# Softmax attention on one core: the value product of a unit behind its four scores, whole instead of in two halves

## The chip, the cores and the metric

The program runs on one core of a Trainium2 chip. The metric is the device time of one execution in microseconds (us). The kernel before took 858.94 us, the median of three runs (858.55 to 862.60). Engines: PE is TensorE, DVE VectorE, ACT ScalarE, POOL GpSimd, SP SyncE, which issues the DMAs.

## The reference, cut to what matters

A two-layer model over x of 2 x 1024 tokens of 128 numbers: linear attention, a mixture of experts, softmax attention, a second mixture. The change lies in the third part:

```
q = rope(x @ Wq.T + bq); k = rope(x @ Wk.T + bk); v = x @ Wv.T + bv     # 16 heads of 8
attn = softmax(q @ k.T / sqrt(8), axis=-1)                               # 1024 x 1024 per head
x = x + (attn @ v) @ Wo.T + bo
```

## The kernel before

The four parts follow each other with a barrier between; the third is `attn1`, one function per engine. It goes through 8 sets (`st`: 2 batches x 4 groups of 4 heads). A **unit** u is one set's block of 128 keys (`kb`, 8 of them) against one half of the queries (`qh`, 512 of them): 16 units a set, 128 in all.

Two streams run side by side.

*Maxima.* For each **tile** (one head, 128 queries) PE multiplies the queries with all 1024 keys in two matmuls of 512 columns into two neighbouring banks (`max_half`, L932), and DVE takes the maximum of the 1024 (`max_tile`, L1063). Even tiles use banks 3 and 4, odd ones 5 and 6; tile n waits until the maximum of n-2 is taken. There are 256 tiles: 22 (`AHEAD`) before the units, then two beside each unit (`tiles_before`), up to unit 116. In the text A and B are the two tiles of a unit, A0, A1, B0, B1 their halves.

*Scores and values.* For each unit PE makes four scores, one per head (`scores`, L961, s0 to s3 in the text), each 128 keys x 512 queries into one bank. The row that carries minus the maximum is part of the operands. ACT takes the exponential into `a1_p` (L1201), which holds three units. Two units later PE multiplies the exponentials with the values (`values`, L974): float32, four heads into four column groups of bank 7, accumulated over the 8 blocks of keys. Each float32 matmul shows as two records, so a call shows as eight. At the first of the 8 blocks PE waits until ACT has copied the last sum out of bank 7 (L1214; ACT does that behind the four exponentials of a unit u with u % 8 = 1, once the product issued in that unit is done).

*Banks of the scores.* Score i of the list `TAKEN` takes bank i % 3 until `FIVE` (the scores of units up to 117), and waits for the exponential that read that bank before (`free_bank`, L937): that of i-3. Behind `FIVE` there are five banks. Once in eight units (u % 8 = 6) the turned rows of maxima (`turn_rows`, L950) take a place in the same list between s1 and s2; ACT copies them (L1192) and a DMA puts them in place.

*Order.* Each engine runs its instructions in the order written. PE's order in a unit is that of the loop at L1003 to L1015: A0 s0 A1 s1, first value half of unit u-2, the turned rows where there are any, B0 s2 B1 s3, second value half. Without tiles (units 117 to 127) it is s0 s1, the whole product, s2 s3. `project_out` (L979) waits for DVE, which turns the outputs (`turn`, `turn_back`) when all maxima are taken. ACT also does a few casts for the last projections (L1141, L1148) behind units 0, 2, 9 and 10.

Of the kernel before, what the change touches and what calls it, by code (L numbers as in the profile page):

```python
# [827 lines left out]
def bank_of(i):  # L828

    return i % 3 if i < FIVE else ((5, 6) + tuple((FIVE + k) % 3 for k in range(3)))[(i - FIVE) % 5]  # L830
# [54 lines left out]
def tiles_before(u):  # L885

    return [n for n in (2 * u + AHEAD, 2 * u + AHEAD + 1) if n < TILES]


def attn1_pe(c):  # L890
# [25 lines left out]
    def max_half(n, half):  # L916
        g, qh, h, qt = tile_at(n)
        k, bank = g % NG, 3 + 2 * (n % 2)
        if half == 0:
            if n == 0:  # L920
                pe.wait_ge(S("a1_b6"), 1)
                pe.wait_ge(S("a1_first"), 3 * 16)
            if n == 1:
                pe.wait_ge(S("a1_b5"), 1)
            if n == 16:
                pe.wait_ge(S("a1_second"), 16)
            if n >= 32 and n % 32 == 0:
                pe.wait_ge(S(f"a1_one{g}"), 3 * 16)
            if n >= 2:
                pe.wait_ge(S("a1_red"), n - 1)  # L930
        rows = slice(S1B, S1B + KR)
        mm = pe.matmul(ps[:, bank + half, :], q[rows, k, qh, h, qt * P:(qt + 1) * P],  # L932
                       kk[rows, k, h, half * BLK:(half + 1) * BLK], start=True, stop=True)
        if half == 1:
            mm.then_inc(S("a1_s1"), 1)

    def free_bank(i):  # L937
        if before_in_bank(i) is not None:
            pe.wait_ge(S("a1_exp"), before_in_bank(i) + 1)
        elif i >= FIVE:  # L940
            pe.wait_ge(S("a1_red"), TILES)

    def turn_rows(e):
        i = TAKEN["rows", e]
        pe.wait_ge(S("a1_split"), e + 1)
        if e == 0:
            pe.wait_ge(S("a1_b4"), 1)
            pe.wait_ge(S("a1_b7"), 1)
        free_bank(i)
        pe.matmul(ps[0:3 * HG * 4, bank_of(i), 0:P], m["a1_ms"][:].rearrange("p i a -> p (i a)"), m["a1_id"][:],  # L950
                  start=True, stop=True).then_inc(S("a1_s2"), 1)

    def scores(u, h):
        st, qh, kb = u // U, u % U // NTB, u % NTB
        k, i = st % NG, TAKEN["score", u * HG + h]
        if h == 0 and u % U == 0:
            pe.wait_ge(S(f"a1_two{st}"), 3 * 16)
        if h == 0 and kb == 0:
            pe.wait_ge(S(f"a1_mrow{qh}"), 16 * (st + 1))
        free_bank(i)  # L960
        pe.matmul(ps[:, bank_of(i), :], kk[0:KA, k, h, kb * P:(kb + 1) * P],  # L961
                  q[0:KA, k, qh, h, :], start=True, stop=True).then_inc(S("a1_s2"), 1)

    def values(u, half=None):
        st, qh, kb = u // U, u % U // NTB, u % NTB
        at = slice(0, BLK) if half is None else slice(half * (BLK // 2), (half + 1) * (BLK // 2))
        if half != 1:
            if kb == 0:
                pe.wait_ge(S("a1_va"), st + 1)
                if u >= NTB:  # L970
                    pe.wait_ge(S("a1_o"), u // NTB)
            pe.wait_ge(S("a1_exp"), TAKEN["score", u * HG + HG - 1] + 1)
        for h in range(HG):
            mm = pe.matmul(ps[32 * h:32 * h + 32, 7, at], va[:, kb, (st % NG) * HG + h, :],  # L974
                           pt[:, (u % 3) * HG + h, at], start=kb == 0 and half != 1, stop=kb == NTB - 1, skip_group_check=True)
        if half != 0:
            mm.then_inc(S("a1_pv"), 1)

    def project_out(b):  # L979
        pe.wait_ge(S("a1_back"), b + 1)  # L980
        pe.wait_ge(S("a1_exp"), max((i + 1 for i in range(FIVE, len(TAKEN)) if bank_of(i) == 3 + b), default=1))
        for j in range(TPB):
            mm = pe.matmul(ps[:, 3 + b, j * D:(j + 1) * D], xnT[:, (b * TPB + j) * P:(b * TPB + j + 1) * P],
                           m["a1_wo"][:], start=True, stop=True)
        mm.then_inc(S("a1_out"), 1)
# [17 lines left out]
    for u in range(G * U):  # L1003
        beside = tiles_before(u)
        for i, n in enumerate(beside or (None, None)):
            for half in range(2):
                if n is not None:
                    max_half(n, half)
                scores(u, 2 * i + half)
            if u >= 2 and (beside or i == 0):  # L1010
                values(u - 2, i if beside else None)
            if i == 0 and u % NTB == NTB - 2 and u + 2 < G * U:
                turn_rows((u + 2) // NTB)
        if u in OUT_UNITS:
            project_out(OUT_UNITS[u])  # L1015
    values(G * U - 2)
# [384 lines left out]
def attn1(c, w, x):  # L1401
    attn1_sp(c)
    attn1_pe(c)
    attn1_act(c, x)
    attn1_dve(c, x)
    attn1_pool(c, x)
    tables_sp(c, w, "f1", 1)
    c.sp.wait_ge(c.sem("n_row"), NT * (c.turn + 1) + TPB)
    c.sp.wait_ge(c.sem("a1_nrow"), 2 * TPB)
    rows_out_sp(c, "f1", 1, range(3))  # L1410
# [1234 lines left out]
```

## Time and profile before

| | before |
|---|---|
| median of the runs | 858.94 us |
| the profiled execution: time | 860.77 us |
| its span, first to last instruction | 859.0 us |
| mean granted clock of TensorE | 0.903 |
| PE busy | 715.8 us (83%) |
| DVE busy | 658.8 us (77%) |
| ACT busy | 526.6 us (61%) |
| POOL busy | 238.3 us (28%) |

The span is the time from the first to the last instruction of the profiled execution; durations in the trace come from it. The units run from about 448 to 752 us. Starts and durations are in us; a row of the timeline merges instructions of one line that follow each other without a gap and gives their number as x2, x3. In brackets stands the idle time of the engine before the row and what ended it. Matmuls are pipelined: the next one starts before the record of the last one ends, so the distance of two starts is the price, not the duration. A granted clock of 1.00 is 2.4 GHz, one of 0.50 is 1.2 GHz.

### The profile page before, as it was taken

How to read it: one execution, taken by the hardware profiler on the slowest of the kernel's cores; microseconds unless marked ns; L12 is line 12 of the kernel's file. 1: busy time of each engine (PE TensorE's matmuls, PEld its weight loads, DVE VectorE, ACT ScalarE, POOL GpSimd, SP SyncE). 2: the span in 40 equal slices, each digit the busy share in tenths (PEclk: the TensorE clock that was granted, in tenths of full speed). 3: DMA queues.
4: the chain of work that ended last, by engine and by line, in shares of the span. 5: the costliest groups of instructions: out<-in, count | busy, mean ns of one | idle time of the engine just before them, and what ended most of it. 6: DMA issues, size and time to landing. Idle time of an engine off the chain costs nothing. (4 is left out here: it accounts for less than half of the span.)

```text
span 859.0 us, 20505 instructions
## 1 busy us (share of the span) xinstructions
PE 715.8 (83%) x8024; PEld 359.3 (42%) x8024; DVE 658.8 (77%) x1317; ACT 526.6 (61%) x1028; POOL 238.3 (28%) x295
## 2 busy tenths in 40 slices
PE   5999978887736999963989999999999999946880
PEld 2333236553426999961412222222222222236770
DVE  7887985446875555537799999999999999664555
ACT  3763622365713444425629999999999999624453
POOL 0130010204216767552473300100000100006773
PEclk9999989997856999985958999999999999767995
DMA  3440010000082311221756650403300000032123
GB/s 101 98 100 3 1 24 5 4 3 1 0 302 95 110 48 50 38 61 60 205 129 148 170 126 2 88 16 75 73 16 2 2 2 9 4 128 84 50 50 101
DMA packets 40968, 55.47 MB, mean 65 GB/s; under 512 B 9210, under 2 KB 31234, under 8 KB 40490
## 3 DMA queue, kind: packets, MB, share of 16 engines
q1 hardware_dynamic: 36906, 46.04, 20.1%
q0 software_dynamic: 3968, 8.13, 3.5%
q8 instruction: 64, 1.05, 0.5%
q14 instruction: 30, 0.25, 0.1%
HBM read 35.22 MB, written 14.55 MB: 58 GB/s over the span
## 5 line engine op out<-in xcount | busy, mean ns | idle before, releaser
L1063 DVE TENSOR_REDUCE arena<-psum 128x1 f32<-128x1024 f32 x256 | 292.8, 1217 | 10.4 <-PE psum L932 10.4
L1201 ACT ACTIVATE arena<-psum 128x512 f32<-128x512 f32 x512 | 276.5, 597 | 18.7 <-PE psum L961 11.4
L932 PE MATMUL psum<-arena 56*128 56x512 bf16 x512 | 164.5, 404 | 4.7 <-DVE arena L1063 3.6
L974 PE MATMUL psum<-arena 128*32 128x256 f32 (+1 forms) x1944 | 163.4, 408 | 5.9 <-issue 5.9
L961 PE MATMUL psum<-arena 59*128 59x512 bf16 x512 | 158.4, 390 | 0.1
L369 PE MATMUL psum<-arena 128*128 128x128 f32 x808 | 108.1, 281 | 0.4 <-DVE arena L420 0.4
L369 PEld LDWEIGHTS psum<-arena 128*128 128x128 f32 x808 | 102.0, 198 | 0.7 <-DVE arena L420 0.7
L974 PEld LDWEIGHTS psum<-arena 128*32 128x32 f32 x1944 | 38.8, 108 | 107.5 <-issue 61.6
L932 PEld LDWEIGHTS psum<-arena 56*128 56x128 bf16 x512 | 28.9, 95 | 115.6 <-DVE arena L1063 97.9
L485 POOL DMA_INDIRECT rows_y<-arena x62 | 62.6, 1009 | 37.7 <-DVE arena L434 31.9
L396 PE MATMUL psum<-arena 128*128 (+1 forms) x496 | 66.5, 277 | 2.8 <-ACT arena L464 2.0
L480 POOL DMA_INDIRECT arena<-rows_x,arena x62 | 60.0, 968 | 26.0 <-issue 17.4
L1273 POOL TENSOR_SCALAR arena<-arena 128x16 f32<-128x16 f32 x16 | 4.1, 254 | 220.4 <-DVE arena L1063 220.3
L396 PEld LDWEIGHTS psum<-arena 128*128 128x128 f32 x496 | 60.3, 192 | 4.8 <-issue 3.3
L461 ACT ACTIVATE arena<-psum 128x512 f32<-128x512 f32 x39 | 23.3, 597 | 44.1 <-PE psum L369 44.1
L453 ACT COPY arena<-arena 128x512 f32 x39 | 24.1, 618 | 32.0 <-PE psum L369 19.4
L2300 PE MATMUL psum<-arena 128*32 128x512 f32 x352 | 41.2, 593 | 0.2 <-DMA arena<-arena 0.2
L424 DVE TENSOR_TENSOR arena<-arena,psum 128x512 f32<-128x512 f32 x39 | 26.8, 687 | 18.4 <-PE psum L369 18.4
L961 PEld LDWEIGHTS psum<-arena 59*128 59x128 bf16 x512 | 30.6, 94 | 17.3 <-ACT arena L1201 14.2
L434 DVE COPY arena<-psum 128x128 f32<-128x128 f32 x62 | 18.1, 292 | 25.0 <-PE psum L396 13.5
L2040 ACT ACTIVATE arena<-psum 128x64 f32<-128x64 f32 x32 | 7.2, 225 | 44.7 <-PE psum L2322 44.7
L417 DVE COPY arena<-arena 128x512 f32 x39 | 17.0, 437 | 19.2 <-issue 16.2
(314 smaller groups left out, 1059.5 us busy)
## 6 DMA issues: line engine op xcount, KB each, us to landing
arena<-scr_q SPq DMA_DIRECT2D x32, 224.0 KB
arena<-scr_k SPq DMA_DIRECT2D x15, 448.0 KB
arena<-in_f_up SPq DMA_DIRECT2D x1, 4096.0 KB, 14.0
arena<-rows_y SPq DMA_DIRECT2D x12, 256.0 KB, 4.8
scr_q<-arena SPq DMA_DIRECT2D x6, 384.0 KB, 5.3
arena<-in_f_down SPq DMA_DIRECT2D x1, 2048.0 KB, 17.0
arena<-in_f_up SPq DMA_DIRECT2D x1, 2048.0 KB, 9.4
rows_x<-xn SPq DMA_DIRECT2D x5, 256.0 KB, 13.0
```

Source lines behind the costliest of these rows:

```text
L369: mm = pe.matmul(ps[:, bank, f * P:(f + 1) * P], w[:, a.pair, at], xt[:, a.pair, :], start=True, stop=True)
L396: mm = pe.matmul(ps[:, 5 + 2 * d.pair, 0:P], h[:, d.pair, f * P:(f + 1) * P], merged(wdown[:, ed, f * P:(f + 1) * P]), start=f == 0, stop= ...
L424: dve.tensor_tensor(h[:, u.pair, :], sg[:, u.pair, :], ps[:, 2 + u.pair, :], ALU.mult).then_inc(hidden, 1)
L453: act.copy(m["e_w"][:, x0.pair, F:2 * F], merged(m["e_up"][:, bass.ds(e, 1), F:2 * F])).then_inc(picked2, 1)
L480: pool.indirect_dma_start(xs[:, t % GATHERED, :], None, src, index).then_inc(landed[t % GATHERED], 16)
L485: pool.indirect_dma_start(dst, index, y[:, d.slot, :], None).then_inc(stored[d.slot], 16)
L932: mm = pe.matmul(ps[:, bank + half, :], q[rows, k, qh, h, qt * P:(qt + 1) * P], kk[rows, k, h, half * BLK:(half + 1) * BLK], start=True, s ...
L961: pe.matmul(ps[:, bank_of(i), :], kk[0:KA, k, h, kb * P:(kb + 1) * P], q[0:KA, k, qh, h, :], start=True, stop=True).then_inc(S("a1_s2"), 1)
L974: mm = pe.matmul(ps[32 * h:32 * h + 32, 7, at], va[:, kb, (st % NG) * HG + h, :], pt[:, (u % 3) * HG + h, at], start=kb == 0 and half != 1 ...
L1063: dve.tensor_reduce(mx[:, qh, h * 4 + qt:h * 4 + qt + 1], ps[:, bank:bank + 2, :].rearrange("p a b -> p (a b)"), X, ALU.max).then_inc(S("a ...
L1201: act.activation(pt[:, (u % 3) * HG + h, :], ps[:, bank_of(i), :], ACT.Exp, scale=float(HD) ** -0.5).then_inc(S("a1_exp"), 1)
L2300: mm = pe.matmul(ps[32 * h:32 * h + 32, fir_bank(n, i), :], m["a0_wfir"][:, (g0 + g) * H0 + h, :], v4[:, h, b, PAD + t0 - 4 * g:PAD + t0 - ...
```

## The change

In the loop of PE the call of `values` moves behind the loop over the two tiles, and it is made without a half. In each unit PE first issues the matmuls of both tiles' maxima and all four scores (with the turned rows between the two tiles, where there are any), then the value product of unit u-2 with 512 columns: four float32 matmuls instead of eight of 256 columns. In the units without maxima the product was whole already; it moves from behind s1 to behind s3. ACT, DVE, POOL and SP are unchanged, and so are all waits.

```diff
@@ -1007,10 +1007,10 @@
                 if n is not None:
                     max_half(n, half)
                 scores(u, 2 * i + half)
-            if u >= 2 and (beside or i == 0):
-                values(u - 2, i if beside else None)
             if i == 0 and u % NTB == NTB - 2 and u + 2 < G * U:
                 turn_rows((u + 2) // NTB)
+        if u >= 2:
+            values(u - 2)
         if u in OUT_UNITS:
             project_out(OUT_UNITS[u])
     values(G * U - 2)
```

## Rows read from the trace of the kernel before

**Rows 1.** The page's groups: line, engine, count | busy us, mean ns | idle before
```profile
L1063 DVE TENSOR_REDUCE arena<-psum 128x1 f32<-128x1024 f32 x256 | 292.8, 1217 | 10.4 <-PE psum L932 10.4
L1201 ACT ACTIVATE arena<-psum 128x512 f32<-128x512 f32 x512 | 276.5, 597 | 18.7 <-PE psum L961 11.4
L932 PE MATMUL psum<-arena 56*128 56x512 bf16 x512 | 164.5, 404 | 4.7 <-DVE arena L1063 3.6
L974 PE MATMUL psum<-arena 128*32 128x256 f32 (+1 forms) x1944 | 163.4, 408 | 5.9 <-issue 5.9
L961 PE MATMUL psum<-arena 59*128 59x512 bf16 x512 | 158.4, 390 | 0.1
```

**Rows 2.** Stretches: window, length, busy per engine (x), granted clock, DMA, GB/s
```profile
573.00:591.40 18.40, 18.02 (x197) 4.55 (x193) 18.21 (x17) 17.88 (x35) 1.09 (x5) 1.00 0.52 102
...
609.80:628.20 18.40, 18.02 (x197) 4.55 (x193) 18.21 (x17) 17.88 (x35) 1.09 (x5) 1.00 0.48 102
```

**Rows 3.** Timeline of PE, unit 72 to the start of 73: start, us, instruction
```profile
615.95 0.39 PE L961 MATMUL psum<-arena 59*128 59x512 bf16 x1
616.17 0.38 PE L961 MATMUL psum<-arena 59*128 59x512 bf16 x1
616.48 0.64 PE L974 MATMUL psum<-arena 128*32 128x256 f32 x8
617.05 0.39 PE L961 MATMUL psum<-arena 59*128 59x512 bf16 x1
...
618.16 0.39 PE L961 MATMUL psum<-arena 59*128 59x512 bf16 x1
```

**Rows 4.** Timeline, ACT and DVE in the same unit: exponential of s0, two maxima
```profile
616.38 0.60 ACT L1201 ACTIVATE arena<-psum 128x512 f32<-128x512 f32 x1
...
615.51 2.35 DVE L1063 TENSOR_REDUCE arena<-psum 128x1 f32<-128x1024 f32 x2
615.51 1.22 DVE L1063 TENSOR_REDUCE arena<-psum 128x1 f32<-128x1024 f32 x1
```

**Rows 5.** Timeline of unit 70, which has the turned rows
```profile
611.27 0.39 PE L961 MATMUL psum<-arena 59*128 59x512 bf16 x1
611.70 1.08 ACT L1201 ACTIVATE arena<-psum 128x512 f32<-128x512 f32 x2
612.20 0.59 ACT L1201 ACTIVATE arena<-psum 128x512 f32<-128x512 f32 x1
612.84 0.09 PEld L961 LDWEIGHTS psum<-arena 59*128 59x128 bf16 x1 [0.19 <-ACT arena L1201]
612.84 0.39 PE L961 MATMUL psum<-arena 59*128 59x512 bf16 x1
613.16 0.64 PE L974 MATMUL psum<-arena 128*32 128x256 f32 x8
613.73 0.39 PE L961 MATMUL psum<-arena 59*128 59x512 bf16 x1
614.37 1.23 DVE L1063 TENSOR_REDUCE arena<-psum 128x1 f32<-128x1024 f32 x1
```

**Rows 6.** Timeline of unit 114: ACT copies bank 7, PE's value half waits
```profile
712.41 0.39 PE L961 MATMUL psum<-arena 59*128 59x512 bf16 x1
712.70 0.59 ACT L1214 COPY arena<-psum 128x512 f32<-128x512 f32 x1
713.17 0.63 ACT L1201 ACTIVATE arena<-psum 128x512 f32<-128x512 f32 x1
713.39 0.64 PE L974 MATMUL psum<-arena 128*32 128x256 f32 x8 [0.38 <-issue]
715.07 0.39 PE L961 MATMUL psum<-arena 59*128 59x512 bf16 x1
```

**Rows 7.** Timeline: s0 of unit 3, s0 of unit 117
```profile
456.72 0.39 PE L961 MATMUL psum<-arena 59*128 59x512 bf16 x1
...
719.50 0.60 PE L961 MATMUL psum<-arena 59*128 59x512 bf16 x2
```

**Rows 8.** Timeline, unit 117: a whole value product; DVE's last maximum
```profile
719.14 1.22 DVE L1063 TENSOR_REDUCE arena<-psum 128x1 f32<-128x1024 f32 x1
720.03 1.06 PE L974 MATMUL psum<-arena 128*32 128x512 f32 x8
721.03 1.03 PE L961 MATMUL psum<-arena 59*128 59x512 bf16 x4
```

**Rows 9.** Timeline, units 10 and 11: ACT's casts for the last projections
```profile
472.76 0.62 ACT L1141 CAST arena<-arena 128x512 bf16<-128x512 f32 x1
473.96 0.64 PE L974 MATMUL psum<-arena 128*32 128x256 f32 x8 [0.90 <-issue]
475.94 0.62 ACT L1148 CAST arena<-arena 128x512 bf16<-128x512 f32 x1
```

**Rows 10.** Timeline of PE in unit 121: the wait for DVE's turned outputs
```profile
731.05 1.16 PE L983 MATMUL psum<-arena,xnT 128*128 128x128 f32 x8 [1.11 <-DVE xnT L1096]
```

**Rows 11.** Stretches (columns as in rows 2): early units, and behind unit 121
```profile
448.00:456.00 8.00, 7.42 (x33) 1.46 (x32) 7.44 (x7) 5.89 (x12) 1.84 (x2) 0.50 0.98 217
456.00:470.00 14.00, 14.00 (x155) 3.71 (x153) 13.81 (x13) 13.67 (x27) 6.07 (x9) 0.99 0.44 116
470.00:480.00 10.00, 9.10 (x104) 2.35 (x96) 9.30 (x9) 9.82 (x20) 2.32 (x2) 1.00 0.90 218
731.00:744.00 13.00, 12.95 (x53) 4.36 (x54) 12.38 (x40) 5.70 (x12) 0.00 (x0) 0.61 0.00 0
```

**Rows 12.** All waits ended by L1201: us in total, times
```profile
PEld psum L974: 45.3, 106
PEld psum L961: 14.2, 28
```

**Rows 13.** Timeline at clock 0.50: score and exponential, whole product and next score
```profile
453.15 0.60 PE L961 MATMUL psum<-arena 59*128 59x512 bf16 x1
453.79 0.60 ACT L1201 ACTIVATE arena<-psum 128x512 f32<-128x512 f32 x1
736.33 1.93 PE L974 MATMUL psum<-arena 128*32 128x512 f32 x8
738.20 0.60 PE L961 MATMUL psum<-arena 59*128 59x512 bf16 x1
```

## The prediction

> **What bounds the kernel now.** I read the page's groups first [rows 1]. Nearly all of the attention stage is five groups: one maximum per tile on DVE (L1063), four exponentials per unit on ACT (L1201), and on PE the matmuls of maxima (L932), scores (L961) and values (L974). The table of stretches [rows 2] shows DVE, ACT and PE all at 97% to 99% of three successive 18.40 us stretches at a granted clock of 1.00, so busy shares can't say which of them sets the pace; the starts can.
>
> One unit of before runs so [rows 3]. A maxima matmul and a score matmul start together (they use different rows of the array), the second pair 0.22 us later, the value half 0.31 after that, and the next pair 0.57 after the half. That is 1.10 to 1.11 us a tile and 2.21 a unit (s0 of unit 72 at 615.95, of unit 73 at 618.16). DVE repeats in 2.35 - 1.22 = 1.13 us, 2.26 a unit, so PE pulls slowly ahead of it. But in each eight units PE loses time twice: the unit with the turned rows lasts 2.46 (611.27 to 613.73, [rows 5]), and the unit behind an output eviction 2.67, since the first half waits for the copy out of bank 7 (712.41 to 715.07, [rows 6]). Six units of 2.21 and these two make 18.4 us (stretches of that length repeat in every count and busy time, [rows 2]); DVE needs only 16 x 1.13 = 18.1 of it. So PE's order of work is the bound now, with DVE 0.3 us in 18.4 behind it and ACT (4 x 0.49 = 1.96 a unit; two that follow at once last 1.08, so the second starts 1.08 - 0.59 = 0.49 behind the first, [rows 5]) farther back. Units 3 to 116 take from 456.72 to 719.50 = 262.8 us [rows 7]. By parts: 86 ordinary x 2.21 + 14 x 2.46 + 14 x 2.67 = 261.9, and 0.5 to 0.6 for the two units beside ACT's last splits.
>
> **PE's own work falls.** Eight value matmuls of 256 columns become four of 512. The price of a whole one stands in the trace, since the units without maxima already use it [rows 8]: 0.31 after the last score it starts, and 1.00 later the next score starts (720.03 to 721.03). PE's work in an ordinary unit is then 3 x 0.23 + 0.31 + 1.00 = 2.00 us against 2.21. By the Trainium skill, "TensorE: Matmul & The Clock Gate", section "Back-to-back issue gap", two gaps of 256 columns (262 cycles each) would equal one of 512 (518), so halving would be free; the rows have 1.00 against 2 x 0.57 and they decide. If PE's own work were all, the unit would drop to DVE's pace.
>
> **What the new order adds is a wait.** Until FIVE the scores use three banks in turn, so score i waits for the exponential of score i-3. With the halves between them, four scores were spread over the unit and only the unit with turned rows waited. Now the fourth score s3 must wait for the exponential of s0 of its own unit, and s0 starts only behind the previous whole product, which stands behind the previous s3. PE works in order, so this is a closed ring, one unit long:
> - s3 to its value product: 0.32 (a score that has waited, 612.84 to 613.16, [rows 5])
> - value product to the next s0: 1.00 [rows 8]
> - s0 to its exponential: 0.43 (615.95 to 616.38, [rows 3, 4])
> - that exponential: 0.60 [rows 4]
> - its end to the score that waits for it: 612.84 - (612.20 + 0.59) = 0.05 [rows 5]
>
> Sum 2.40 us a unit. It is longer than PE's work (2.00) and DVE's pace (2.26), so it sets the pace. s3 would be ready 0.68 after s0 and starts 1.08 after it.
>
> Behind the waiting s3 on PE are the whole value product and then both maxima of the next unit; DVE waits for those. B1 is ahead of s3 and isn't held up. A ring over DVE exists too: B0, B1 0.23, values 0.31, next A0 1.00, its maximum 0.64 (lead of A0 over its reduction, 713.73 to 714.37, [rows 5]), the next 1.13, that one's 1.22 and 0.05 of release: 4.58 over two units, 2.29 each, under 2.40. ACT's wait for a free third of a1_p (values of u-3) ends 1.06 + 0.04 behind the start of the previous product, while the new s0's result is there 1.43 behind it: hidden by 0.3.
>
> **The two special units.** Turned rows take a bank too, so in these 14 units (6, 14, ... 110) s3 waits for the exponential of s1: 0.43 + 0.49 + 0.59 + 0.05 = 1.57 behind s0, which is just where it stands today (611.27 to 612.84, [rows 5]). Then 0.32 + 1.00: the unit lasts 2.89 (before 2.46). The turned rows' own matmul lies inside that wait. ACT copies bank 7 once in eight units (14 times), behind the last exponential of a unit and the end of the product. Now the copy starts 1.06 + 0.04 behind that product's start, the next exponential 0.47 later (712.70 to 713.17, [rows 6]), takes 0.63, releases in 0.05, and 0.32 on is the next product: 2.57 us in that unit (before 2.67). PE's own wait for the copy disappears, as it ends 1.7 behind the product and the next product is 2.57 behind it. The two units where ACT splits the last projections [rows 9] cost 0.5 and 0.1 more than their likes today; on the new ring I take 0.5 in all (bounds 0 and 1.2).
>
> **Sum.** 86 x 2.40 + 14 x 2.89 + 14 x 2.57 + 0.5 = 206.4 + 40.5 + 36.0 + 0.5 = 283.4 against 262.8: +20.6 us.
>
> **Ends of the stage.** The first three units: at the low clock (0.50 up to 456 us, [rows 11]) unit 2 waits on PE in both orders; I take nothing (bounds -0.5 to 1.5). In the last eleven units there were whole products before; they now follow four scores, not two, with five banks, so no score waits for the one three before it, and PE's work of 1.97 is the same. They are covered by DVE, which turns eight outputs after its last maximum before PE may go on: PE waits 1.11 us there [rows 10]. That chain starts with the last maximum, 0.36 ahead of s0 of unit 117 today (719.14, 719.50, [rows 7, 8]) and, on the new ring, 0.62 ahead: -0.3. Then comes a stretch in which the granted clock falls to 0.50 after that pause [rows 11]; 13.0 us at 0.61 on average hold some 10 us at the lower level, so not falling would give back up to 5 us. The new pause is some 0.6 us, shorter, but one of 0.90 went by without a fall [rows 9, 11] and one of 1.11 did not. I keep the fall, and the 5 us as the range's lower end. Nothing behind the stage changes.
>
> The profiled execution has a span of 859.0 and a time of 860.77, the median of the runs shown is 858.94. +20.6 - 0.3 = +20.3 gives a span of 879.3 and, on the median, 879.2 us.
>
> **Rivals.**
> *The ring doesn't close* (not slower). If s3 found its bank free in time, PE would need 2.00 and DVE's ring of 2.29 would be the pace: 114 x 2.29 = 261.1, that is -1.7 us, 857 us; were even that slack, 114 x 2.26 = 257.6, -5.2, 854 us. It decides if the release of the bank comes within 0.68 us of s0 and not 1.08: an exponential would have to last 0.20 us, not 0.60 [rows 4], or the bank would have to come from elsewhere. Against it: the same wait stands in 28 scores today, 14.2 us [rows 12]. For it: only that the prices of different places are added. Chance 0.09 (0.07 for 857, 0.02 for 854).
>
> *The clock falls inside the loop.* PE now pauses about 0.2 us before B0 and 0.2 before s3 in each unit. At the lower level the ring would be 0.56 + 1.87 + 0.65 + 0.60 + 0.05 = 3.73 us, or about +150 us over the loop, some 1,010 to 1,030. The product's 1.87 is 736.33 to 738.20, the lead 0.65 is 453.15 to 453.79 [rows 13]. Against it: pauses of 0.38 in each 18.4 us and one of 0.90 left the clock at 1.00 [rows 2, 6, 11]. The Trainium skill, same page, "A second HAM failure mode: psum-queue depth-cycling", says that matmuls of 512 columns cycling through banks, with short pauses between groups, can make the clock swing; by that rule this rival would be the result, and no stretch of the loop shows it so far. Chance 0.03.
>
> *The clock holds in the tail.* Same ring, less up to 5 us: about 874.5. Chance 0.15.
>
> *The order puts ACT behind.* Four scores arrive in a burst; the exponentials start 0.43, 0.92, 1.41 and 1.90 behind s0, the last ends at 2.5, and the next unit's first can start at 2.83. So 0.3 of slack; if it were gone (an exponential kept back by a read of a bank beside PE's writes), each 0.05 is 5.7 us. Chance 0.05, at 885.
>
> **How the numbers follow.** Forecast, ring of 2.40 with the fall in the tail: 0.68, 879.2 us. Its own errors: 0.02 on the ring's sum is 2.3 us. The range 873.5 to 884.5 takes in the held clock, 0.83 in all. A measurement of this kernel can tell about 0.5% (4.3 us). Faster by more: 0.02; within: 0.07; slower: 0.91.
>
> **What would show it.** Right: s0 to s0 of 2.40 in ordinary units, 2.89 and 2.57 in the special ones; s3 1.08 behind s0, its weight load idle before it and released by L1201 in some 110 units, not 28; L974 with 1024 matmuls of 512 columns and no 256; DVE idle some 0.13 us in each unit, released by PE; 16 tiles in 19.8 us, not 18.4. Wrong: s3 0.68 behind s0 with DVE without gaps (the first rival), or a granted clock under 1.00 between 460 and 735 us (the second). If the unit is longer than 2.40 with s3 released by L1201 as said, ACT's start is the term to look at.

## The result and the profile after

The changed kernel takes 878.79 us (median of four runs, 878.0 to 879.97), the kernel before 858.75 beside it (four runs). The ratio is 1.0229, 95% interval 1.0191 to 1.0267: slower by 2.3% (1.9 to 2.7%), some 20 us. Forecast were 879.2 us, in a range of 873.5 to 884.5.

The profiled execution of after has a span of 877.1 us and a time of 879.04. The page's groups of after, beside [rows 1]:

```profile
L1063 DVE TENSOR_REDUCE arena<-psum 128x1 f32<-128x1024 f32 x256 | 301.1, 1219 | 23.8 <-PE psum L932 19.8
L1201 ACT ACTIVATE arena<-psum 128x512 f32<-128x512 f32 x512 | 265.5, 604 | 45.3 <-PE psum L961 45.1
L961 PE MATMUL psum<-arena 59*128 59x512 bf16 x512 | 170.6, 390 | 3.4 <-ACT arena L1201 0.6
L974 PE MATMUL psum<-arena 128*32 128x512 f32 x1024 | 137.4, 609 | 0.0
L961 PEld LDWEIGHTS psum<-arena 59*128 59x128 bf16 x512 | 38.1, 94 | 62.0 <-ACT arena L1201 57.6
```

The busy time of the value matmuls falls from 163.4 to 137.4 us: PE really has less to do. But the weight loads of the scores now have 62.0 us of idle time before them, nearly all released by the exponentials, and both DVE and ACT wait for PE more than before (23.8 and 45.3 us against 10.4 and 18.7). The timeline of one ordinary unit of after (60), PE and ACT, shows the wait itself, beside [rows 3, 4]:

```profile
599.02 0.39 PE L961 MATMUL psum<-arena 59*128 59x512 bf16 x1
599.25 0.38 PE L961 MATMUL psum<-arena 59*128 59x512 bf16 x1
599.45 0.60 ACT L1201 ACTIVATE arena<-psum 128x512 f32<-128x512 f32 x1 [0.33 <-PE psum L961]
599.67 0.09 PEld L961 LDWEIGHTS psum<-arena 59*128 59x128 bf16 x1
599.90 0.38 PE L932 MATMUL psum<-arena 56*128 56x512 bf16 x1
600.10 0.09 PEld L961 LDWEIGHTS psum<-arena 59*128 59x128 bf16 x1 [0.32 <-ACT arena L1201]
600.42 1.06 PE L974 MATMUL psum<-arena 128*32 128x512 f32 x8
601.42 0.39 PE L961 MATMUL psum<-arena 59*128 59x512 bf16 x1
```

s0 starts at 599.02, its exponential at 599.45, and ends at 600.05; s3, whose partner B1 (L932) had started at 599.90, starts at 600.10; the whole product at 600.42; the next s0 at 601.42. These are the five terms of the ring: 0.43, 0.60, 0.05, 0.32, 1.00, in all 2.40. The unit with the turned rows (62; beside [rows 5]):

```profile
603.82 0.39 PE L961 MATMUL psum<-arena 59*128 59x512 bf16 x1
604.90 0.39 PE L961 MATMUL psum<-arena 59*128 59x512 bf16 x1
605.39 0.39 PE L961 MATMUL psum<-arena 59*128 59x512 bf16 x1
605.71 1.06 PE L974 MATMUL psum<-arena 128*32 128x512 f32 x8
606.71 0.39 PE L961 MATMUL psum<-arena 59*128 59x512 bf16 x1
```

s3 is 1.57 behind s0, and the unit lasts 2.89. And the unit behind the copy out of bank 7 (66; PE's lines and ACT's, beside [rows 6]): the product waits for nothing of its own any more, the copy delays the first exponential instead (0.62 behind s0, not 0.43), and with it s3 (1.27).

```profile
613.90 0.39 PE L961 MATMUL psum<-arena 59*128 59x512 bf16 x1
614.03 0.58 ACT L1214 COPY arena<-psum 128x512 f32<-128x512 f32 x1
614.52 0.60 ACT L1201 ACTIVATE arena<-psum 128x512 f32<-128x512 f32 x1
615.17 0.39 PE L961 MATMUL psum<-arena 59*128 59x512 bf16 x1
615.49 1.06 PE L974 MATMUL psum<-arena 128*32 128x512 f32 x8
616.49 0.39 PE L961 MATMUL psum<-arena 59*128 59x512 bf16 x1
```

Where the 18.1 us between the two spans (877.1 - 859.0) lie, by the starts of s0:

| stretch | before | after | difference |
|---|---|---|---|
| up to unit 0 | 448.54 | 447.60 | -0.9 |
| units 0 to 2 | 8.18 | 8.66 | +0.5 |
| units 3 to 116 | 262.78 | 284.22 | +21.4 |
| units 117 to 123 | 21.66 | 17.39 | -4.3 |
| from unit 124 to the end | 117.83 | 119.28 | +1.4 |

The last row isn't explained by the change. In the kernels below, in which nothing behind unit 124 was changed either, that stretch differs by 2 us on like chips (129.8 to 132.1).

### The profile page after: what moved, and what is told of

It is laid out like the page before. It is cut to its first block and busy times, and to the rows that moved or that the text cites. A ratio compares the mean times of both kernels' runs of the same rounds, so it can differ in the third digit from the quotient of the medians.

```text
span 877.1 us, 18665 instructions
## 1 busy us (share of the span) xinstructions
PE 735.6 (84%) x7104; PEld 353.9 (40%) x7104; DVE 666.8 (76%) x1317; ACT 515.8 (59%) x1028; POOL 238.3 (27%) x295
## 3 DMA queue, kind: packets, MB, share of 16 engines
q1 hardware_dynamic: 36906, 46.04, 19.5%
## 5 line engine op out<-in xcount | busy, mean ns | idle before, releaser
L1063 DVE TENSOR_REDUCE arena<-psum 128x1 f32<-128x1024 f32 x256 | 301.1, 1219 | 23.8 <-PE psum L932 19.8
L1201 ACT ACTIVATE arena<-psum 128x512 f32<-128x512 f32 x512 | 265.5, 604 | 45.3 <-PE psum L961 45.1
L961 PE MATMUL psum<-arena 59*128 59x512 bf16 x512 | 170.6, 390 | 3.4 <-ACT arena L1201 0.6
L932 PE MATMUL psum<-arena 56*128 56x512 bf16 x512 | 162.7, 406 | 8.2 <-DVE arena L1063 3.7
L974 PE MATMUL psum<-arena 128*32 128x512 f32 x1024 | 137.4, 609 | 0.0
L369 PEld LDWEIGHTS psum<-arena 128*128 128x128 f32 x808 | 103.4, 201 | 0.7 <-DVE arena L420 0.7
L932 PEld LDWEIGHTS psum<-arena 56*128 56x128 bf16 x512 | 31.5, 96 | 171.0 <-DVE arena L1063 144.9
L961 PEld LDWEIGHTS psum<-arena 59*128 59x128 bf16 x512 | 38.1, 94 | 62.0 <-ACT arena L1201 57.6
L396 PEld LDWEIGHTS psum<-arena 128*128 128x128 f32 x496 | 60.8, 193 | 4.7 <-issue 3.2
L461 ACT ACTIVATE arena<-psum 128x512 f32<-128x512 f32 x39 | 23.3, 597 | 44.4 <-PE psum L369 44.4
L453 ACT COPY arena<-arena 128x512 f32 x39 | 24.1, 618 | 32.1 <-PE psum L369 19.5
L2300 PE MATMUL psum<-arena 128*32 128x512 f32 x352 | 41.2, 593 | 0.2 <-DMA arena<-arena 0.2
L424 DVE TENSOR_TENSOR arena<-arena,psum 128x512 f32<-128x512 f32 x39 | 26.8, 687 | 18.7 <-PE psum L369 18.7
L434 DVE COPY arena<-psum 128x128 f32<-128x128 f32 x62 | 18.1, 291 | 26.1 <-PE psum L396 13.9
L974 PEld LDWEIGHTS psum<-arena 128*32 128x32 f32 x1024 | 20.3, 108 | 32.0 <-issue 25.3
L464 ACT ACTIVATE arena<-arena 128x512 f32<-128x512 f32 x23 | 14.5, 630 | 29.5 <-DVE arena L428 29.5
```

The lines of the kernel that those rows point to most:

```text
L369: mm = pe.matmul(ps[:, bank, f * P:(f + 1) * P], w[:, a.pair, at], xt[:, a.pair, :], start=True, stop=True)
L396: mm = pe.matmul(ps[:, 5 + 2 * d.pair, 0:P], h[:, d.pair, f * P:(f + 1) * P], merged(wdown[:, ed, f * P:(f + 1) * P]), start=f == 0, stop= ...
L424: dve.tensor_tensor(h[:, u.pair, :], sg[:, u.pair, :], ps[:, 2 + u.pair, :], ALU.mult).then_inc(hidden, 1)
L453: act.copy(m["e_w"][:, x0.pair, F:2 * F], merged(m["e_up"][:, bass.ds(e, 1), F:2 * F])).then_inc(picked2, 1)
L1063: dve.tensor_reduce(mx[:, qh, h * 4 + qt:h * 4 + qt + 1], ps[:, bank:bank + 2, :].rearrange("p a b -> p (a b)"), X, ALU.max).then_inc(S("a ...
L1201: act.activation(pt[:, (u % 3) * HG + h, :], ps[:, bank_of(i), :], ACT.Exp, scale=float(HD) ** -0.5).then_inc(S("a1_exp"), 1)
```

## Experiments

"Loop" is s0 of unit 3 to s0 of unit 117 in the trace, "eight units" from unit 88 to 96. The kernel before takes 885.4 to 886.5 us on the chips of e1 to e8b and of e11, more than in the first comparison (858.75) and on the chip of e9 and e10 (858.04), so ratios and stretches are what can be compared, not medians. Its loop isn't known on the slower chips, but the one kernel in its order with full maxima, e2, has the same 263.0 us; what is longer lies outside the loop (s0 of unit 0 starts at 460 to 472 us there, and 130 to 132 us follow s0 of unit 124). e6b, e7b, e8b and e10 are one execution each; their loops are compared by their traces. The edits of e2, e3, e8b and e9 are shown against the kernel before, the others against the changed one; "..." stands for lines left out.

### Which part of the change costs

**e1_loop_only** keeps the order of before in the units without maxima:

```diff
+            if u >= 2 and not beside and i == 0:
+                values(u - 2)
...
-        if u >= 2:
+        if u >= 2 and beside:
             values(u - 2)
```

> The change in the units with maxima alone (0 to 116); the last eleven units keep the order of before, with the whole product behind s1. Ring theory: 2.40 us in ordinary units, the loop from s0 of unit 3 to s0 of unit 117 as in the changed kernel, 284 us against 263, so about +21 us: 876 to 885 us, the upper end if the granted clock falls behind unit 121 as it did before. Rival, that the loss comes from the last units or from elsewhere in the program: under 865 us.

903.86 us against 885.98, ratio 1.0201 (1.0147 to 1.0256). Loop 283.3 us, units of 2.40, 2.89 and 2.59. The loss lies in the loop.

**e2_tail_only** is the opposite: halves as before in the loop, the product behind four scores from unit 117 on.

```diff
-            if u >= 2 and (beside or i == 0):
-                values(u - 2, i if beside else None)
+            if u >= 2 and beside:
+                values(u - 2, i)
...
+        if u >= 2 and not beside:
+            values(u - 2)
```

> The change in the last eleven units alone: the loop with maxima keeps its halves, from unit 117 on the whole product stands behind all four scores. Theory: no ring of consequence (five banks from unit 118 on), the loop stays at 263 us; PE's pause before the first output projection shrinks from 1.11 us to about 0.7 us, since unit 117 still has three banks and lasts 0.4 us longer, and if the clock holds over it, as it did in the changed kernel, 3 to 4.5 us are gained: 854 to 856 us. Rival, that the held clock came from the ring's order in the loop: no change, 858 to 860 us.

885.09 us against 885.98, ratio 0.9979 (0.9952 to 1.0007): no difference that can be told, and no sign of the 3 to 4.5 us forecast. Loop 263.0 us, units 117 to 123 in 17.6. PE's pause was 0.95 us, not 0.7; the clock held. Why a held clock gained so little shows in e10.

### Place or width

**e3_between** puts the whole product between the two tiles, two scores on each side:

```diff
-            if u >= 2 and (beside or i == 0):
-                values(u - 2, i if beside else None)
+            if u >= 2 and beside and i == 0:
+                values(u - 2)
...
+        if u >= 2 and not beside:
+            values(u - 2)
```

> The whole product between the two tiles: A0 s0 A1 s1, product, B0 s2 B1 s3, so that no four scores come in one burst; last units as in the changed kernel. Ring theory: between two whole products there are four scores whatever the place, and three banks, so one score waits for the exponential of the score behind the last product; here it is s1 that waits for the exponential of s2 of the unit before: s2 to exponential 0.43, exponential 0.60, release 0.05, s1 to product 0.32, product 1.00 = 2.40 us again, total 877 to 882 us. Rival, that it is the burst of four scores or the place behind s3 that costs: two scores on each side of the product as before, DVE's pace of 2.26 to 2.30 us, 855 to 862 us.

909.34 us, ratio 1.0242 (1.0194 to 1.029); ordinary units 2.40 from s1 to s1 (the score that waits; from s0 to s0 they vary from 2.3 to 2.7), eight units 20.06, loop 286.3. It is 2 us more than in the changed kernel, since here the product waits for the copy out of bank 7 as before: that unit lasts 3.10. The burst of four scores isn't what costs. Between two whole products there are four scores wherever the product stands, and three banks. PE's timeline has the ring at its other place: s1 of the unit is now the one that starts late (696.36, with A1 at 696.15).

```profile
695.92 0.39 PE L961 MATMUL psum<-arena 59*128 59x512 bf16 x1
696.15 0.38 PE L932 MATMUL psum<-arena 56*128 56x512 bf16 x1
696.36 0.39 PE L961 MATMUL psum<-arena 59*128 59x512 bf16 x1
696.67 1.07 PE L974 MATMUL psum<-arena 128*32 128x512 f32 x8
697.67 0.39 PE L961 MATMUL psum<-arena 59*128 59x512 bf16 x1
```

**e4_halves_behind** leaves the width and changes the place alone:

```diff
-        if u >= 2:
+        if u >= 2 and beside:
+            values(u - 2, 0)
+            values(u - 2, 1)
+        elif u >= 2:
             values(u - 2)
```

> The place alone: the product stays in two halves of 256 columns, but both stand behind the four scores. Ring theory: the same ring with the price of two halves in a row, which lies between 1.00 (as a whole one) and 2 x 0.57 = 1.14: 2.40 to 2.54 us a unit, 879 to 895 us. Rival, that the width of 512 columns costs and not the place: 858 to 862 us.

907.16 us, ratio 1.0212 (1.0162 to 1.0262). Ordinary units 2.402, eight units 19.90 in place of 19.87. PE, one unit: s3, both halves, next s0.

```profile
697.18 0.39 PE L961 MATMUL psum<-arena 59*128 59x512 bf16 x1
697.50 1.07 PE L974 MATMUL psum<-arena 128*32 128x256 f32 x16
698.51 0.39 PE L961 MATMUL psum<-arena 59*128 59x512 bf16 x1
```

Two halves in a row take 1.01 us, a whole one 1.00. The whole loss is the place's. The 0.14 us that a whole product saves against 2 x 0.57 comes from having one block of value matmuls between scores instead of two, not from the width.

### What the ring is made of

**e5b_short_exp** shortens one term, ACT's:

```diff
-            act.activation(pt[:, (u % 3) * HG + h, :], ps[:, bank_of(i), :], ACT.Exp, ...
+            act.activation(pt[:, (u % 3) * HG + h, 0:BLK // 2], ps[:, bank_of(i), 0:BLK // 2], ACT.Exp, ...
```

> One term of the ring made shorter: the order of the changed kernel, but ACT takes each exponential over 256 of the 512 columns (the other half of the weights is left out, it keeps what lay there). PE, DVE and the banks are as changed. An exponential falls from 0.60 to some 0.37 us (the copies of 512 and of 128 columns, 0.59 and 0.25, give 0.09 us for 100 columns). Ring theory: 2.40 - 0.23 = 2.17, now under DVE's pace of 2.26 and the ring over DVE of 2.29, so an ordinary unit lasts 2.26 to 2.29 us and eight units some 18.2 to 18.6 in place of 19.87: about 20 us back, near the kernel before. Rival, that PE's order or the reduction of maxima holds the pace: still 2.40.

887.55 us against 886.48, ratio 1.0033 (0.9997 to 1.007). The exponential lasts 0.38 us. Eight units take 18.53, the loop 264.7: 19.5 us come back for 0.22 us less in the one exponential of each unit that lies in the ring. ACT's own amount of work can't be the reason, as ACT waits in most units here (the second row below: 0.87 us before a pair of exponentials) and waited in the changed kernel too. The gain is less than 114 x 0.22 = 25, since DVE catches the pace: its reductions now follow with next to no gap (five in 5.80 us, where 4 x 1.13 + 1.22 = 5.74 is the least), and PE waits for them ahead of B0 (last two rows; the matmul's label names the exponential, which ends at the same 672.31 as the reduction and for which B0 doesn't wait in the code). The ordinary units aren't even, 2.19 to 2.40, as the ring over DVE spans two of them; their mean is 2.29, the prediction's figure for that ring.

```profile
671.09 5.80 DVE L1063 TENSOR_REDUCE arena<-psum 128x1 f32<-128x1024 f32 x5
671.93 0.66 ACT L1201 ACTIVATE arena<-psum 128x256 f32<-128x256 f32 x2 [0.87 <-PE psum L961]
672.36 0.09 PEld L932 LDWEIGHTS psum<-arena 56*128 56x128 bf16 x1 [0.74 <-DVE arena L1063]
672.36 0.39 PE L932 MATMUL psum<-arena 56*128 56x512 bf16 x1 [0.25 <-ACT arena L1201]
```

**e6b_one_bank** takes DVE off the pace, **e7b_five_banks** gives the freed banks to the scores:

```diff
-        k, bank = g % NG, 3 + 2 * (n % 2)
+        k, bank = g % NG, 3 + 2 * (n % 2) - half
...
-                          ps[:, bank:bank + 2, :].rearrange("p a b -> p (a b)"), X, ALU.max)
+                          ps[:, bank, :], X, ALU.max)
```

and, in e7b only (with a longer look back in `before_in_bank`),

```diff
-    return i % 3 if i < FIVE else ...
+    return (0, 1, 2, 4, 6)[i % 5] if i < FIVE else (5, 6, 0, 1, 2)[(i - FIVE) % 5]
```

> The order of the changed kernel with DVE taken off the pace: both maxima matmuls of a tile write into one bank and DVE reduces 512 columns instead of 1024 (the maximum over the first half of the keys is left out). Scores keep three banks. Ring theory: DVE's part drops to some 0.6 us a tile and nothing changes in the loop: 2.40, 2.89 and 2.59 us a unit, 19.9 us for eight. Rival, that DVE's two-unit ring of 2.29 with its waits makes up part of the 2.40: under 2.35.

908.26 us; loop 283.4, eight units 19.87, the same to 0.01 us as with the full reduction (0.68 us instead of 1.22).

> The kernel of e6b with one thing more: banks 4 and 6, now unused by maxima, go to the scores, which then have five in turn instead of three. The same part of the maxima is left out. Ring theory: the fourth score waits for nothing, and the unit falls to PE's own work of 2.00 or ACT's 4 x 0.48 to 0.49 = 1.96: 2.00 to 2.05 us a unit, 16 to 16.6 us for eight, the loop some 45 us shorter than in e6b. Rival, that not the banks but the work behind the scores costs: stays at 2.40.

852.03 us; units of 1.97, eight units 16.19, loop 231.9. Five banks for three make each ordinary unit 0.43 us shorter with the same work on every engine, and the unit with the turned rows falls from 2.89 to 2.24. PE in e6b, s0 to s3 and the product, then the same of e7b:

```profile
686.37 0.39 PE L961 MATMUL psum<-arena 59*128 59x512 bf16 x1
686.59 0.38 PE L961 MATMUL psum<-arena 59*128 59x512 bf16 x1
686.81 0.38 PE L961 MATMUL psum<-arena 59*128 59x512 bf16 x1
687.45 0.39 PE L961 MATMUL psum<-arena 59*128 59x512 bf16 x1
687.76 1.07 PE L974 MATMUL psum<-arena 128*32 128x512 f32 x8
```

```profile
645.39 0.39 PE L961 MATMUL psum<-arena 59*128 59x512 bf16 x1
645.61 0.38 PE L961 MATMUL psum<-arena 59*128 59x512 bf16 x1
645.83 0.38 PE L961 MATMUL psum<-arena 59*128 59x512 bf16 x1
646.05 0.38 PE L961 MATMUL psum<-arena 59*128 59x512 bf16 x1
646.35 1.06 PE L974 MATMUL psum<-arena 128*32 128x512 f32 x8
647.35 0.39 PE L961 MATMUL psum<-arena 59*128 59x512 bf16 x1
```

s3 is 1.08 behind s0 in the one and 0.66 in the other; nothing else in the unit moves by more than 0.02 us.

**e8b_one_bank_halves** is e6b's edit on the kernel before, and asks what bounded that one.

> The control for e6b in the order of the kernel before: halves between the scores, three banks, DVE reduces 512 columns from one bank (the same part of the maxima is left out). PE is the bound there: 2.21, 2.46 and 2.67 us a unit as before, 18.4 for eight, so 21 us under e6b. If DVE's pace were the bound of the kernel before, eight units would fall towards 17.7.

885.61 us; loop 262.79, eight units 18.41: equal to the kernel before to 0.01 us, though each reduction lasts 0.69 us and not 1.22. DVE, 99% busy in [rows 2] (18.21 of 18.40 us), had no part in the pace. It now waits for PE before each reduction:

```profile
670.43 0.69 DVE L1063 TENSOR_REDUCE arena<-psum 128x1 f32<-128x512 f32 x1 [0.41 <-PE psum L932]
```

### Versions that might be better, and the clock in the last units

**e9_late_half** keeps the halves, but moves the first behind s2 in the one unit of eight that waits for the copy; the last units as in e2.

```diff
                 scores(u, 2 * i + half)
+                if u >= 2 and beside and u % NTB == 2 and (i, half) == (1, 0):
+                    values(u - 2, 0)
-            if u >= 2 and (beside or i == 0):
-                values(u - 2, i if beside else None)
+            if u >= 2 and beside and not (u % NTB == 2 and i == 0):
+                values(u - 2, i)
...
+        if u >= 2 and not beside:
+            values(u - 2)
```

> A version that may beat both: the halves of the kernel before, but in the one unit of eight in which the product waits for ACT's copy out of bank 7 the first half moves from behind s1 to behind s2; last eleven units as in the changed kernel. Theory: the copy ends 0.89 us behind s0, PE does B0 and s2 at 0.45 meanwhile, so that unit lasts some 2.43 in place of 2.67 us, eight units 18.17 (DVE's own 16 x 1.13 = 18.1 is the floor), the loop 3.3 us shorter, 259.5. Nothing is left out. Ratio to before 0.994 to 0.998. Rival, that the wait only moves, because B1 comes later and DVE starves: 18.4 again, no change.

855.66 us against 858.04 (12 and 17 runs), ratio 0.9983 (0.9963 to 1.0003): the same. The unit didn't shrink: 2.72 in place of 2.67, eight units 18.46, loop 264.3 where 259.5 were forecast (1.0 of the 264.3 is unit 3, which lasts 3.26 here, as the granted clock rose only at 462.6, behind its start at 460.2). My figure let B0 start 0.45 behind s0; it starts 0.93 behind, at 662.90. B0 needs the bank of the tile two before, whose maximum DVE, at that point nearly one tile behind PE, takes until 0.88. So PE stands still before B0 instead of before the half. The rival had the outcome right: the wait only moved, from a value half to a maximum, by DVE's banks, which I had counted in the ring over DVE and left out here. The weight load of B0 names DVE; the matmul's own label names the copy (L1218), which ends within 0.02 us of that maximum (both at 662.85) and for which B0 doesn't wait in the code.

```profile
661.97 0.39 PE L961 MATMUL psum<-arena 59*128 59x512 bf16 x1
662.19 0.38 PE L932 MATMUL psum<-arena 56*128 56x512 bf16 x1
662.90 0.09 PEld L932 LDWEIGHTS psum<-arena 56*128 56x128 bf16 x1 [0.82 <-DVE arena L1067]
662.90 0.39 PE L932 MATMUL psum<-arena 56*128 56x512 bf16 x1 [0.33 <-ACT arena L1218]
663.22 0.64 PE L974 MATMUL psum<-arena 128*32 128x256 f32 x8
663.80 0.39 PE L961 MATMUL psum<-arena 59*128 59x512 bf16 x1
```

**e10_before_again** is the kernel before, unchanged.

> The kernel before once more, unchanged, for its last eleven units. In the first trace the granted clock fell behind unit 121 (PE's pause 1.11 us) and that stretch cost 4 us more than in five other kernels, whose pauses were 0.69 to 0.98 us. If the fall hangs on the order of work or on a pause over 1 us, it comes again with the same pause, units 117 to 124 in 21.7 us; if it hangs on the execution, the clock holds and they take 17.5 us. The loop is 262.8 us either way.

855.47 us, span 854.1, loop 262.9. The pause before the first output projection is again 1.11 us, yet the clock held, and units 117 to 123 take 17.75 us, not 21.7. The stretches of e10 (first row) and of the trace before for the same stage (second row), columns as in [rows 2]; the granted clock is the third number from the end:

```profile
728.00:744.00 16.00, 14.89 (x97) 4.63 (x90) 15.06 (x46) 13.34 (x27) 0.00 (x0) 1.00 0.04 7
```

```profile
729.00:745.00 16.00, 14.89 (x68) 4.69 (x64) 15.01 (x46) 8.70 (x18) 0.00 (x0) 0.68 0.04 7
```

The same program with the same pause had both outcomes, so the order of work alone doesn't decide the fall. What does is open. Two executions can't say how often the kernel before has it, nor whether a shorter pause makes it rarer.

**e11_one_matmul** is e7b without the maxima matmuls that nothing reads there.

```diff
+        if half == 0:
+            return
         rows = slice(S1B, S1B + KR)
```

> The kernel of e7b (order of the changed kernel, scores in five banks, DVE reduces one bank of 512 columns), now also without the maxima matmuls over the first half of the keys, which DVE never read there; timed against the kernel before. What is left out is the maximum over the first 512 keys; it only keeps the exponentials in range, the weights are the same without it. Theory: 1.97 us a unit is ACT's four exponentials (4 x 0.49) as much as PE's work, so taking matmuls out that run beside the scores changes nothing in the loop (16.2 us for eight units), and the ratio to before stays near e7b's 852.03 / 886.48 = 0.961. If PE's matmuls of maxima had a price of their own beside the scores, the loop would be shorter still.

849.69 us against 885.37, ratio 0.9592 (0.956 to 0.9625). Loop 232.4, eight units 16.25: nothing gained over e7b. Alone this doesn't show that the matmuls of maxima are free, as ACT's exponentials (4 x 0.49 = 1.96) could hide a gain. The starts say it: four scores with no maxima beside them start (1.03 - 0.39) / 3 = 0.21 apart [rows 8], in e7b with one beside each 0.22. This version is 4.1% faster than the kernel before. It rests on leaving half of the keys out of the maximum, which these inputs allow; no run has inputs whose second half of keys would not bound the scores, and with them the exponentials could overflow. Five banks in the order of the kernel before were not run; PE's own work is 2.21 a unit there and none of its ordinary units waits for a bank, so by my estimate five banks alone would leave them at 2.21, and the 1.97 needs the new order as well.

## Why the prediction was right, point by point

*PE is the bound of the kernel before, DVE isn't.* Shown by e8b: half the reduction, the same loop of 262.79 us.

*A whole product costs 1.00 and PE's work falls to 2.00 a unit.* Right: 600.42 to 601.42, and e7b's 1.97, where the scores start 0.22 apart without a wait. But I set 1.00 against 2 x 0.57 and let that overrule the other reading, that halving the width is free. e4 shows that it is free for two halves in a row (1.01); the 0.14 is the price of a second block.

*The ring of 2.40.* Each of the five terms stands in the trace of after at its forecast value to 0.01 us. Three things show that it is this ring and not a loss that happens to be as large: the place doesn't matter as long as four scores lie between products (e3), a shorter exponential gives the time back (e5b), and two more banks take the wait away (e6b to e7b).

*Special units:* 2.89 forecast and found; 2.57 forecast, 2.59 found (the exponential that follows a copy starts 0.49 behind it, not 0.47). The two units beside ACT's last splits cost 0.44 more than their likes, 0.5 forecast.

*The loop:* 283.4 forecast, 284.2 found. The 0.8 us too few are nearly all unit 3, which takes 3.21 us (s0 at 456.26 and 459.47): the clock was still at its lower level there (second matmuls of 0.63 us), where in the kernel before it had risen by 456.7. Units 0 to 2 cost 0.5 more, within the bounds given.

*The tail.* This step was wrong. I kept the fall of the clock in the last units, and it didn't come: units 117 to 123 take 4.3 us less than in the first trace, where -0.3 was forecast for the whole tail. PE's pause was 0.71 where some 0.6 was forecast. So the rival at 0.15 had the mechanism, but its 874.5 us are not what came. It took the slow stretch of one profiled execution (860.77 us) as part of the kernel before's usual time, and so did I; e10, the same program at 855.47, has no fall. Against e10 a held clock leaves 17.39 against 17.75, some 0.4. Why the clock held in the changed kernel isn't known.

*The total.* That 878.79 lies 0.4 from the 879.2 forecast is in part luck. By spans the difference is 18.1 us against the first trace (20.3 forecast: loop +21.4 for +20.6, tail -4.3 for -0.3, +1.0 elsewhere for nothing) and 23.0 against e10; the 20.0 between the medians lie between the two. What isn't luck is the loop.

*DVE idle 0.13 us in each unit:* right. It is idle for 23.8 us in all, 10.4 before, so 13.4 us more in 114 units, 0.12 in each. *Scores that wait for exponentials:* 140 loads against some 110 forecast and 28 before [rows 12]: s3 in each of the 117 units with maxima, and s2 in the 14 with turned rows, which I had left out; the other nine are single ones.

*The clock falling inside the loop* didn't happen: the row below has 1.00 over 480 to 735 us, though PE stands some 0.2 us ahead of s2 in five of eight units and again ahead of s3 (they start 0.65 and 1.08 behind s0, where e7b has 0.44 and 0.66). The Trainium skill's page "TensorE: Matmul & The Clock Gate", in "A second HAM failure mode: psum-queue depth-cycling", reports a kernel with cycling banks and short pauses in which it swings. The trace doesn't agree for this kernel.

```profile
480.00:735.00 255.00, 249.57 (x1657) 52.05 (x1657) 241.44 (x207) 219.91 (x437) 21.50 (x70) 1.00 0.19 41
```

## What to carry to other kernels

Before work on an in-order engine is gathered into one block, count the buffers that the other stream fills between two blocks. With n of them and more than n fills, one fill waits for a reader that can only start behind the last block. The period is then block + hand-over + reader + hand-over, if that is longer than what each engine needs by itself. That sum can be made from five rows of the kernel before. A busy share doesn't give it: DVE at 99% said nothing about the pace here, as halving its work changed nothing. A stretch that was slow in one execution is to be looked up in a second before it is counted as part of the time.

## What the runs showed of the hardware

The granted clock fell to its lower level in the last units in one of two executions of the same program with the same pause of 1.11 us. In eight other kernels with a pause of 0.48 to 1.00 us there, and in three with 0.30 us or none, it held. Two accumulating matmul groups of 256 columns in a row cost the same as one of 512 (1.01 and 1.00 us), while each block of its own costs something: two separated halves make PE's unit 2 x 0.57 + 2 x 0.23 + 2 x 0.31 = 2.22 us, one block 1.00 + 3 x 0.23 + 0.31 = 2.00. Going once more from scores (59 rows, bf16) to values (128 rows, float32) and back thus costs 0.22 us, 0.08 of it before the product and 0.14 in it; whether the rows, the type or the column groups make it, no run separates. And a matmul of 56 rows that runs beside one of 59 rows costs at most 0.01 us: scores start 0.21 us apart without it and 0.22 with it.
